# Half of the q evictions on VectorE, fewer increments in the output projection and a shorter wait ahead of the expert layers

## The reference, cut to what matters

```python
xn = _layernorm(x)                       # x: (2, 8192, 1024)
# attention between the 4 heads of one token, not between tokens
q = (xn @ Wq + bq).reshape(b, s, 4, 1024); k, v alike
scores = (einsum('bshd,bsgd->bshg', q*cos, k*cos)
        + einsum('bshd,bsgd->bshg', q*sin, k*sin)) / 32
out = einsum('bshg,bsgd->bshd', softmax(scores), v)
s = swapaxes(out, 1, 2).reshape(b, s, 4096) @ Wo + bo
# 8 experts, the best 2 of them per token
y_e = silu(xn @ W1[e].T) @ W2[e].T
g = silu(sum_e gate[e] * y_e)
x = x + s * g
```

## Time and profile before

| | us |
|---|---|
| median of 3 runs | 5979.2 (fastest 5967.09) |
| profiled execution, its own time | 5966.42 |
| span of its slowest core (core 5) | 5964.9 |
| spans of the 8 cores | 5941.0 to 5964.9 |
| start of the last bias matmuls, the end of attention | 2083.43 |
| start of the first expert matmul (L825) | 2192.82 |

### The profile page before, as it was taken

One profiled execution on the slowest core, in us unless ns is written; L12 is line 12 of the kernel. 1 busy time (PEld: TensorE's weight loads), 2 busy tenths in 40 slices (PEclk: granted clock), 3 DMA queues, 4 the chain that ended last, 5 costly groups with the idle time before them and its releaser, 6 DMA issues.

```text
span 5964.9 us, 57247 instructions; the slowest of 8 cores (5941.0 to 5964.9 us)
## 1 busy us (share of the span) xinstructions
PE 4980.1 (83%) x22368; PEld 2196.9 (37%) x22368; DVE 1515.1 (25%) x1928; ACT 1136.6 (19%) x1991; POOL 370.6 (6%) x678
## 2 busy tenths in 40 slices
PE   4856874884786545999999999999999999999990
PEld 2222222322322222444444444444444444444440
DVE  1641434245053312111211111111111111111113
ACT  2310220131012044111111111111111111111111
POOL 0000000000000010100100100100001001001000
PEclk9788886877978767999999999999999999999995
DMA  5325432632642340311311311311212212213104
GB/s 100 57 50 97 87 64 39 117 57 37 107 75 50 55 101 18 57 29 29 57 29 29 57 29 29 57 29 33 53 29 41 45 29 48 38 29 55 31 1 137
DMA packets 138918, 314.33 MB, mean 53 GB/s; under 512 B 13474, under 2 KB 50594, under 8 KB 126370
## 3 DMA queue, kind: packets, MB, share of 16 engines
q0 software_dynamic: 121520, 268.50, 25.9%
q1 hardware_dynamic: 17138, 42.18, 2.2%
HBM read 566.50 MB, written 12.58 MB: 97 GB/s over the span
## 4 chain that ended last, share of the span: by engine, by line
PE 78%; DVE 7%; DMA 7%; ACT 4%; issue 3%; SPq 0%; DVEq 0%; ACTq 0%; POOLq 0%
PE PD L825 30%; PE PD L856 30%; PE PD L307 10%; DVE AB L549 4%; PE PD L445 4%; PE PD L612 3%; DMA wor<-wo_h 3%; DMA wpan<-wk_p 2%; ACT vt_st L510 1%; DMA s_stg<-s_scr 1%; DVE prod L433 1%; PE PB L519 1%; PE PD L288 1%; DMA wpan<-wq_p 1%; DVE AB L542 0%
## 5 line engine op out<-in xcount | busy, mean ns | idle before, releaser
L825 PE MATMUL PD<-AB 128*128 128x512 bf16 x8192 | 1794.1, 380 | 0.0
L868 DVE SCALAR_TENSOR_TENSOR AFr<-PD,gate,AFr 128x1024 f32<-128x1024 f32 x512 | 657.2, 1284 | 2857.1 <-PE PD L856 2857.1
L832 ACT ACTIVATE AB<-PD 128x512 bf16<-128x512 f32 x1024 | 611.5, 597 | 2893.9 <-PE PD L825 2893.9
L825 PEld LDWEIGHTS PD<-AB 128*128 128x128 bf16 x8192 | 801.5, 98 | 971.0 <-issue 7.0
L856 PE MATMUL PD<-wpan,AB 128*128 128x512 bf16 x4096 | 894.5, 379 | 0.0
L307 PE MATMUL PD<-xnT_f,wpan 128*128 128x512 bf16 x3072 | 734.9, 396 | 73.6 <-DMA wpan<-wq_p 35.9
L856 PEld LDWEIGHTS PD<-wpan,AB 128*128 128x128 bf16 x4096 | 401.3, 98 | 482.8
L856 PE MATMUL PD<-xnT_f,AB 128*128 128x512 bf16 x2048 | 483.8, 379 | 0.0
L307 PEld LDWEIGHTS PD<-xnT_f,wpan 128*128 128x128 bf16 x3072 | 302.2, 101 | 444.0 <-issue 143.6
L433 DVE SCALAR_TENSOR_TENSOR prod<-AB,wcl 128x512 bf16<-128x512 bf16 x512 | 346.3, 745 | 248.8 <-ACT AB L418 158.2
L612 PE MATMUL PD<-wor,AB 128*128 128x512 bf16 x1024 | 273.5, 430 | 110.4 <-DMA wor<-wo_h 87.6
(11 more groups left out here) (85 smaller groups left out, 1443.7 us busy)
## 6 DMA issues: line engine op xcount, KB each, us to landing
AB<-w1t POOLq DMA_DIRECT2D x256, 256.0 KB, 13.2
wpan<-wk_p POOLq DMA_DIRECT2D x32, 1024.0 KB, 8.9
wpan<-wq_p POOLq DMA_DIRECT2D x32, 1024.0 KB, 8.0
wpan<-wv_p POOLq DMA_DIRECT2D x32, 1024.0 KB, 7.9
wor<-wo_h POOLq DMA_DIRECT2D x64, 512.0 KB, 6.4
wpan<-w2t POOLq DMA_DIRECT2D x128, 256.0 KB, 7.0
xnT_f<-w2t POOLq DMA_DIRECT2D x64, 256.0 KB, 4.9
x_st<-xr SPq DMA_DIRECT2D x24, 512.0 KB, 4.5
```

Of the source, the lines that this page charges most:

```text
L825: last = S.emit("pe", lambda e, lhs=lhs, dc=dc, pp=pp, g=g: e.matmul(PD[0][:, pp * 512:pp * 512 + 512], lhs, xnT_ffn[:, dc * 2048 + g * 51 ...
L832: e_sil = S.emit("act", lambda e, fc=fc, pp=pp: e.activation(hT[:, fc * 512:fc * 512 + 512], PD[0][:, pp * 512:pp * 512 + 512], AF.Silu), ...
L868: e.scalar_tensor_tensor(acc[:, t16 * 1024:t16 * 1024 + 1024], PD[bi][:], gate[:, t16 * 8 + ex:t16 * 8 + ex + 1], acc[:, t16 * 1024:t16 * ...
```

## The change

It makes three edits. The evictions of the odd q chunks move from ACT to DVE. In the output projection only the last of the 16 matmuls of a weight load raises the semaphore, where every fourth did. And the transposes ahead of the experts wait for the last eviction of the output projection alone, no longer for the last spill.

```diff
-                        e_q2 = S.emit("act", lambda e, nc_idx=nc_idx, sub=sub, pp=pp: e.activation(
-                            qbT[:, sub * 512:sub * 512 + 512],
-                            PD[0][:, pp * 512:pp * 512 + 512], AF.Identity,
-                            bias=bqc[:, nc_idx:nc_idx + 1]), after=[e_mm], ms=True)
+                        if sub % 2 == 0:
+                            e_q2 = S.emit("act", lambda e, nc_idx=nc_idx, sub=sub, pp=pp:
+                                          e.activation(
+                                qbT[:, sub * 512:sub * 512 + 512],
+                                PD[0][:, pp * 512:pp * 512 + 512], AF.Identity,
+                                bias=bqc[:, nc_idx:nc_idx + 1]), after=[e_mm], ms=True)
+                        else:
+                            e_q2 = S.emit("dve", lambda e, nc_idx=nc_idx, sub=sub, pp=pp:
+                                          e.tensor_scalar_add(
+                                qbT[:, sub * 512:sub * 512 + 512],
+                                PD[0][:, pp * 512:pp * 512 + 512],
+                                bqc[:, nc_idx:nc_idx + 1]), after=[e_mm], ms=True)
...
-                                    ms=(h == 3))
+                                    ms=(h == 3 and sub == 3))
...
-                                              extra_after=ffn_guard + list(xpd2))
+                                              extra_after=[group_wo_done] + list(xpd2))
```

## The result

The ratio of the changed kernel to the one before is 1.0105, 95% interval 1.0055 to 1.0155: slower, and within the band of 2%. It is 6003.2 us for the changed kernel (17 such dies) and 5956 to 5958 us for the kernel before in the three sets of runs that came with the experiments (20, 9 and 12 dies): 45 to 47 us more.

A forecast was written before the change was run, and what follows sets the result against it. In the score stage PE sets the pace during projections and DVE during products. 48.3 + 3 + 0 + 0 = 51 us on 5966.4 gives 6017.7, with the median allowance 6022; 6002 to 6040 holds 0.80, the 8-in-10 range 6000 to 6046.

The forecast's parts named there:

- The first term: Score stage: four products per head move from beside the projections to behind chunk 7's DVE eviction; 3.02 us a head, 48.3 us.
- the head start: Score stage: four products DVE made beside each head's projections before the change; losing them was put at 2.65 us a head.
- the 0.36 us a head: Score stage: part of the 3.02 us a head put on the products' later start behind the last DVE eviction.
- The clock term: Mid-group projections: PE's granted clock could return earlier or later after the product phase; +3 us, bounds -12 to +18.
- Increments and the spill wait: Output projection's 192 fewer increments, and the expert transposes' dropped wait for the last spill: each put at 0 us.
- The sum: Whole kernel: 48.3 + 3 + 0 + 0 = 51 us on the profiled 5966.4 us, giving 6017.7 us.
- 0 to 13 us more for a median: Whole kernel: allowance for a median lying above the profiled execution, taking the forecast from 6017.7 to 6022 us.
- Shared evictions that free PE: Rival, q projection: 64 evictions off ACT hand back 44 us of PE time; 5970 us, 5983 as median; chance 0.05.
- The head start of no worth: Rival, score stage: only the last eviction's 0.36 us a head stays, 6 us; 5972 us, median to 5985; chance 0.04.
- The clock gone wrong in every head: Rival: mid-group projections cost 16.45 us instead of about 15, products slower; 6043 us, median up to 6056; chance 0.10.

The follow-up runs named there:

- e5_wait_last_q: Kernel before, all evictions on ACT, but every product of a head waits for chunk 7's eviction; ratio 1.0073, core mean 6006.3 us against 5958.0.
- e3_products_between: Changed kernel with the first four products of a head queued on DVE between its evictions; core mean 5961.9 us, +4 on the kernel before.
- e1_q_only: Kernel before with only the odd q evictions moved to DVE, without the other two edits; core mean 6001.7 us against 5958.0, +44.
- e2_rest_only: Kernel before with only the fewer increments and the dropped spill wait, q evictions unmoved; core mean 5956.2 us against 5958.0, -2.
- e10_delay_2048: Kernel before with one unneeded 128x2048 DVE memset ahead of the scaling of the scores; core mean 5956.1 us against 5955.9.
- e11_delay_4096: Kernel before with one unneeded 128x4096 DVE memset ahead of the scaling of the scores; ratio 1.000, core mean 5960.1 us against 5955.9.
- e7_all_increment: Kernel before with every output projection matmul raising the semaphore, 1024 increments instead of 256; core mean 5960.6 us against 5957.7, +3.
- e9_pipelined_shared: As e8_pipelined, but with the odd q chunks evicted by DVE; ratio to the kernel before 0.9687, core mean 5774.9 us against 5957.7.
- e8_pipelined: Kernel before with the score stage rebuilt chunk by chunk, 12 product buffers, score matmuls two chunks behind, q evictions on ACT; ratio 0.9632.

## Why the prediction was right or wrong

- **The first term, 48.3 us: right, in each step.** The eviction starts with PE's last matmul, the first product 0.67 us later, 32 products take 21.28 us, and the part of a head behind its projections is 2.98 us longer (forecast 3.02), 48 us in all. e5_wait_last_q and e3_products_between show that the head start is the cause and not the eviction work, e1_q_only and e2_rest_only that the other edits have no part in it. For the 0.36 us a head that I put on the eviction itself, the product parts of e3_products_between show 0.33. That its total came out at 4 us for the 6 forecast is luck, since its projections lost 4 us and its V stages gave back 9.
- **The clock term, +3 us: hit by luck where I put it, and absent where the clock moved most.** The trace could not decide between -12 and +18 us, and I took the middle. The projections in mid-group got 0.32 us longer each, 4 us in all. But the low level reaches on into the V stage, which I had never opened, and so put at nothing without a reason. There the changed kernel got 2.5 us a group back, 10 us in all. e10_delay_2048 and e11_delay_4096 show that a later start of that stage can do this without any change to the score stage.
- **Increments and the spill wait, 0: right**, by e2_rest_only, and by e7_all_increment in the other direction. The Trainium skill (TensorE: Matmul & The Clock Gate, The cost: per-tile semaphore tail) gives 26.3 ns an increment for tiles that run concurrently. By that figure e7_all_increment would be an estimated 20 us slower. It measured +3 and an unchanged pace of 0.216 us, so the figure does not carry over to full-array matmuls one after the other.
- **The sum.** 51 us forecast on the profiled execution, 43 there and 45 to 47 in the core means. The V stage's 10 us, which the forecast did not have, account for the gap. The ratio's 1.0105 is 63 us, with an interval of 33 to 93.
- **The step that failed is the last one, "0 to 13 us more for a median".** I took the distance between the profiled execution and a median of three runs as the spread of the measurement. The changed kernel's median lies 70 us above its own profiled execution; for the kernel before, the median over ten runs lies 121 us above. So 6079.8 falls outside 6000 to 6046, and outside the narrower 6002 to 6040 that the prediction gives for the same chance. The profiled execution (6009.4) and the time that the ratio gives on it (5966.4 x 1.0105 = 6029) lie inside both. The three runs that I had of the kernel before showed it already: one of them took 6208.56 us, and the range had no room for it.
- **The rivals.** Shared evictions that free PE: not seen anywhere. The Trainium skill (TensorEngine Tiling (Array Packing), PSUM Bottleneck) says to use both engines where, after a speedup of TensorE by tiling, the copy out of PSUM may become the bottleneck. That condition, which the prediction leaves out, is not met here: PE did not wait for PSUM (a chunk every 1.727 us), and e9_pipelined_shared lost some 33 us to e8_pipelined by sharing. The head start of no worth: refuted by e5_wait_last_q. The clock gone wrong in every head: refuted by the projections of the second to fourth heads, 15.2 us in the mean for the 16.45 of that rival.

## What to carry to other kernels

Low busy shares on two engines are no proof of room where the engines take turns: ask which engine sets the pace in each phase, and what it did for nothing in the other engine's phase. Before moving an instruction to another engine, look at what stands behind it in that engine's queue; 64 evictions cost some 45 us ahead of the products and 4 us between them. When the timeline shows turns, overlap them: the same instructions, chunk by chunk and with each panel waited for alone, gave 3.7%. And when an experiment's total is small, look at its stages: here two shifts of the clock cancelled the 5 us that it was meant to show.

## What the runs showed of the hardware that I had not expected

A delay can be nearly free. 2.0 or 4.1 us of idleness more ahead of the V stage shortened that stage by 2.2 or 3.9 us, since fewer of its matmuls ran at the 1.2 GHz level. What decides when the clock comes back is not shown by these runs. They show that the length of a stage behind a low phase can change by 4 us when the work ahead of it shifts. In the two delay kernels and the changed kernel the shift was the same in every group and core read; in e5_wait_last_q it came in 12 groups of 20. A few microseconds of difference in a stage that was not touched are no evidence of a mechanism in it.
